# Router products turned over and spread on four column groups, the second routing stage rearranged between engines, two sets of FFN accumulators

## The chip, the core and the metric

The kernel runs on one core of a Trainium2 chip. Its time is the device time of one execution in microseconds (us), from several runs; a profile of one more execution gives a trace with the start and duration of every instruction. The engines are PE (TensorE, matrix products), DVE (VectorE), ACT (ScalarE), POOL (GpSimd) and SP (SyncE, which here only issues DMA transfers). PEld is PE's weight load.

## The reference

```python
x = L0_attn_x                                   # 8 x 1024 x 256
x = x + 0.5 * _L0_ffn_ref(_layernorm(x), router_w, w1, w2)
x = x + _L0_attn_ref(_layernorm(x), Wq, bq, Wk, bk, Wv, bv, Wp, bp)   # 16 heads of 16, rope, causal
x = x + 0.5 * _L0_ffn_ref(_layernorm(x), router_w, w1, w2)

def _L0_ffn_ref(x, router_w, w1, w2):           # 8192 tokens, 8 experts of capacity 1024
    logits = x_flat @ router_w
    expert_idx = argmax(softmax(logits)); gate = the probability of that expert
    pos = running count of tokens of the same expert; keep = pos < 1024
    expert_in[expert_idx, pos] += x_flat * keep
    hidden = gelu(expert_in @ w1[e]); expert_out = hidden @ w2[e]
    return expert_out[expert_idx, pos] * gate * keep
```

## The kernel before, in words

Five stages follow each other, each a block that all engines enter and leave together: first routing (`first_route_block`, names `r1_`), first FFN (`ffn_block`, `f1`), attention (`attention_block`, `at_`), second routing (`second_route_block`, `r2_`), second FFN (`f2`). Each engine runs its own program; semaphores order them. The trace writes `r_` and `f_` for either stage. A batch is 1024 tokens (8 tiles of 128); there are 8 batches, and a quarter q of a batch is two tiles.

**Routing.** For a batch b, DVE's `measure` takes mean and variance, POOL's `invert_std` finds 1/std by Newton steps, `normalize` writes `xn`, PE transposes it (`xt_ps`), ACT copies that to `xt`, and PE's `router(b, q)` multiplies: xt as the stationary operand, router_w (8 columns) moving, four fp32 products a quarter. DVE's `choose` picks the expert, PE's `count` makes running counts, DVE's `place_rows` computes the row number of each token and signals `rows_ready`, and POOL's `scatter(b)` sends the 8 tiles with an indirect DMA each to `expert_in`.

**Second routing** does the attention's output projection first. Attention leaves unnormalised outputs and their sums in DRAM (`o_rows`). At its start the sums of all batches are loaded (L588), inverted (L838) and stored (L593); then per batch SP's `load_o(b)` (L577) brings 1 MB of outputs to `o_in[b % 2]`, `load_inverses(b)` (L585) brings the inverses, each repeated over 16 rows, to the one buffer `o_inv`, POOL's `scale(b)` (L610) multiplies the two, ACT's `high` (L717) and DVE's `low` (L763) split the product into two fp32r parts for each half batch, PE's `project` (L655) multiplies, and DVE's `add` (L769) adds to x. `load_inverses(b)` waits for `scale(b - 1)`, `load_o(b)` for both `low` of batch b - 2. In the loop over b the work on batches b + 2 and b + 3 (add, low, scale) stands between the steps of routing for b and b - 1: POOL's order is `invert_std(b + 1)`, `scale(b + 3)`, `scatter(b - 1)`. DVE's `normalize` (L793) is there too.

**FFN.** 16 blocks of 512 rows, two an expert. In a block, for f in 0..7, PE runs `up(b, f)` (six products into `hid_ps`, L1084), ACT gelu and the high part, DVE the low part (L1037), and PE, two steps later, `down(b, f)` (twelve products into four accumulators `y_ps`, L1099). DVE's `combine(b)` (L1015) reads the accumulators after the block's last `down`; it stands in DVE's program after the low part f = 1 of the next block, and PE's first `down` of the next block waits for it:

```python
                pe.wait_ge(hid_lo_ready, FC * b + f + 1)
                if f == 0 and b >= 1:
                    pe.wait_ge(y_ready, b)
```

**Attention** runs 32 groups (four a batch), 12 steps t each, with PE, DVE (row maxima, L1525 and L1528) and ACT (exponentials) in a ring of three PSUM banks.

Of the kernel before, what the change touches and what calls it, by code (L numbers as in the profile page):

```python
# [14 lines left out]
F32 = mybir.dt.float32  # L15
# [13 lines left out]
E, CAP, F = 8, 1024, 1024  # L29
FC = F // P  # L30
# [165 lines left out]
def first_route_block(nc, sh, dr, w):  # L196
# [6 lines left out]
    with ExitStack() as ctx:  # L203
# [17 lines left out]
        xt = [sb(f"xt{k}", [P, TPQ, CC, P], F32) for k in range(2)]  # L221
# [14 lines left out]
        logit_ps = [ps(f"logit_ps{k}", [P, TPB, E]) for k in range(2)]  # L236
# [4 lines left out]
        x_loaded = [sem(f"x_loaded{b}") for b in range(B)]  # L241
# [8 lines left out]
        xt_used = sem("xt_used")  # L250
# [11 lines left out]
        def _(sp):  # L262
            def load_x(b):
                sp.dma_start(sh.x[:, TPB * b:TPB * (b + 1), 0:C],
                             dr["x"][b * S:(b + 1) * S, :].rearrange("(t p) c -> p t c", p=P)
                             ).then_inc(x_loaded[b], 16)
# [6 lines left out]
            sp.dma_start(sh.router[:], dr["router_w"].rearrange("(c p) e -> p c e", p=P)).then_inc(constants_loaded, 16)  # L273
# [44 lines left out]
        def _(pe):  # L318
            def router(b, q):
                n = QPB * b + q  # L320
                pe.wait_ge(xt_ready, n + 1)
                if q == 0 and b >= 2:
# [22 lines left out]
            for b in range(B):  # L345
                for q in range(QPB):
# [9 lines left out]
                    if q >= 1:  # L356
                        router(b, q - 1)
                    if q == 2 and b >= 1:
                        count(b - 1)
                router(b, QPB - 1)  # L360
# [3 lines left out]
        def _(act):  # L364
            def exponentials(b):
# [5 lines left out]
            for b in range(B):  # L371
                for q in range(QPB):
                    n = QPB * b + q
                    act.wait_ge(xt_ps_ready, n + 1)
                    if n >= 2:
                        act.wait_ge(xt_used, n - 1)
                    nc.scalar.copy(xt[q % 2][:], xt_ps[q % 2][:]).then_inc(xt_ready, 1)
                if b >= 1:
                    exponentials(b - 1)
            exponentials(B - 1)  # L380
# [3 lines left out]
        def _(dve):  # L384
# [15 lines left out]
            def measure(b):  # L400
                m, at = b // 2, per_pair * (b // 2) + 2 * (b % 2)
                dve.wait_ge(x_loaded[b], 16)
# [24 lines left out]
            def choose(b):  # L427

                k = b % 2
                dve.wait_ge(xt_used, QPB * (b + 1))  # L430
                link(v.tensor_reduce(best[:], logit_ps[k][:], AX.X, ALU.max))
                if b >= 2:
                    dve.wait_ge(exp_ready, b - 1)
                v.tensor_tensor(less[k][:], logit_ps[k][:], wide(best), ALU.subtract).then_inc(less_ready, 1)
# [53 lines left out]

def second_route_block(nc, sh, dr, w):
# [6 lines left out]
    with ExitStack() as ctx:  # L496
# [18 lines left out]
        half = [sb(f"half{k}", [P, TPB], F32) for k in range(2)]  # L515
        bits = sb("bits", [P, TPB], I32)
# [3 lines left out]
        sums = xn[:].rearrange("p a j c -> p (a j c)")  # L520
        assert TOK * H == P * 2 * TPQ * C
        xt = [sb(f"xt{k}", [P, TPQ, CC, P], F32) for k in range(2)]
        less = [sb(f"less{k}", [P, TPB, E], F32) for k in range(2)]
        work = [sb(f"work{k}", [P, TPB, E], F32) for k in range(2)]
        hot = sb("hot", [P, TPB, E], F32)
        onehot = [sb(f"onehot{k}", [P, TPB + 1, E], BF16) for k in range(2)]
        counts = sb("counts", [P, TPB, E], F32)
# [10 lines left out]
        logit_ps = [ps(f"logit_ps{k}", [P, TPB, E]) for k in range(2)]  # L538
# [22 lines left out]
        xt_used = sem("xt_used")  # L561
# [11 lines left out]
        def _(sp):  # L573
# [14 lines left out]
            sp.dma_start(sums, dr["o"].rearrange("(n v) t -> n v t", v=VW)[:, D, :]).then_inc(sums_loaded, 16)  # L588
            sp.dma_start(wp[:], dr["wp_t"].rearrange("(c p) o -> p c o", p=P)).then_inc(wp_loaded, 16)
            load_o(0)  # L590
            load_o(1)
            sp.wait_ge(sums_inverted, 1)
            sp.dma_start(dr["inv_sums"], sums).then_inc(sums_stored, 16)  # L593
            sp.wait_ge(sums_stored, 16)
# [1366 lines left out]
```

## Time and profile before

| | us |
|---|---|
| median of three runs (lowest to highest) | 2720.24 (2717.07 to 2720.41) |
| the profiled execution's own time | 2707.74 |
| its span, first to last instruction | 2706.0 |
| first routing | 0 to 145.9 |
| first FFN and attention | 145.9 to 2010.0 |
| second routing | 2012.2 to 2275.7 |
| second FFN | 2275.7 to 2706 |
| PE, DVE, ACT, POOL busy | 2227.9, 1699.0, 1218.6, 966.9 |

How to read it: a stage ends when its slowest engine does, so busy shares over the whole span say little; each stage has its own limit. Durations that this text uses come from the profiled execution.

### The profile page before, as it was taken

To read this page: it belongs to the slowest core of one execution; us is meant where nothing else is said; L and a number is where in the kernel's file an instruction comes from. 1 tells how busy PE (TensorE), PEld (TensorE's weight loads), DVE (VectorE), ACT (ScalarE), POOL (GpSimd) and SP (SyncE) were. 2 spreads that over 40 slices of the span, in tenths; PEclk is the share of its full clock that TensorE was granted. 3 is DMA by queue.
4 is the path that set the end of the run, shared out by engine and by line. 5 is a ranking of instruction groups with operands and counts; after the bars stand their busy time and mean duration, and the time that the engine had idled before them with its cause. 6 is when DMAs were issued, how large, how long until landed. Compare 5 with 4: busy or idle time off the path is not lost. (4 is left out here: it accounts for less than half of the span.)

```text
span 2706.0 us, 43185 instructions
## 1 busy us (share of the span) xinstructions
PE 2227.9 (82%) x14740; PEld 1451.9 (54%) x14740; DVE 1699.0 (63%) x5181; ACT 1218.6 (45%) x2442; POOL 966.9 (36%) x1344
## 2 busy tenths in 40 slices
PE   6659999935699999999999999999962664899997
PEld 6658888834334444444444444443322664788886
DVE  7435555433477877877878878877733663555552
ACT  1224444411056665665666665666750212344443
POOL 3723434326423333333333333330002564333442
PEclk9999999965589999999999999999986775999999
DMA  9552223021524434435344344344315424323220
GB/s 341 187 197 96 88 71 104 29 73 58 132 64 110 117 84 111 112 86 130 87 110 114 86 97 111 80 105 99 80 60 124 144 69 165 126 71 100 77 71 22
DMA packets 185131, 283.21 MB, mean 105 GB/s; under 512 B 14392, under 2 KB 147704, under 8 KB 176720
## 3 DMA queue, kind: packets, MB, share of 16 engines
q1 hardware_dynamic: 170576, 247.08, 34.0%
q0 software_dynamic: 14336, 33.38, 3.5%
q8 instruction: 117, 1.92, 0.3%
q14 instruction: 102, 0.84, 0.1%
HBM read 153.99 MB, written 126.88 MB: 104 GB/s over the span
## 5 line engine op out<-in xcount | busy, mean ns | idle before, releaser
L1646 ACT ACTIVATE at_probs<-at_score_ps 128x512 f32<-128x512 f32 (+3 forms) x1536 | 692.9, 497 | 451.6 <-PE at_score_ps L1763 312.6
L1525 DVE CUSTOM_DVE_ANT_0 at_junk<-at_max_ps,at_causal 128x128 f32<-128x128 f32 (+3 forms) x1024 | 485.5, 484 | 128.2 <-PE at_max_ps L1749 126.2
L1749 PE MATMUL at_max_ps<-at_k,at_q 96*128 96x512 bf16 (+3 forms) x1536 | 494.1, 341 | 43.1 <-DVE at_peak L1525 30.7
L1760 PE MATMUL at_score_ps<-at_q,at_k 99*128 99x512 bf16 (+3 forms) x1536 | 499.3, 332 | 10.7 <-DMA at_v<-v_rows 4.4
L1528 DVE TENSOR_REDUCE at_peak<-at_max_ps 128x1 f32<-128x512 f32 x512 | 352.4, 688 | 118.2 <-PE at_max_ps L1749 114.9
L1037 DVE TENSOR_TENSOR f_hid_lo<-f_hid,f_hid_hi 128x512 fp32r<-128x512 f32 x256 | 177.5, 693 | 322.8 <-ACT f_hid_hi L1061 322.2
L1749 PEld LDWEIGHTS at_max_ps<-at_k,at_q 96*128 96x128 bf16 x1536 | 144.6, 98 | 398.0 <-DVE at_peak L1525 192.0
L1058 ACT ACTIVATE f_hid<-f_hid_ps 128x512 f32<-128x512 f32 x256 | 153.3, 599 | 413.7 <-PE f_hid_ps L1084 413.5
L1773 PE MATMUL at_o_ps<-at_probs,at_v 128*32 128x512 f32 (+3 forms) x3072 | 337.8, 512 | 1.2 <-ACT at_probs L1646 0.7
L1099 PE MATMUL f_y_ps<-f_w_hi,f_hid_hi 128*128 128x256 f32 x1024 | 292.7, 286 | 47.4 <-DVE f_xe L1015 28.9
L1099 PE MATMUL f_y_ps<-f_w_hi,f_hid_lo 128*128 128x256 f32 x1024 | 291.4, 285 | 0.0
L1099 PE MATMUL f_y_ps<-f_w_lo,f_hid_hi 128*128 128x256 f32 x1024 | 290.2, 283 | 0.0
L960 POOL TENSOR_SCALAR f_xn<-f_xe 128x256 f32<-128x256 f32 x120 | 164.3, 1376 | 217.3 <-PE f_xt_ps L1072 168.0
L1099 PEld LDWEIGHTS f_y_ps<-f_w_hi,f_hid_hi 128*128 128x128 f32 x1024 | 194.2, 190 | 70.4 <-issue 41.2
L1368 POOL TENSOR_TENSOR at_by_cos<-at_qk,at_cos 128x512 f32<-128x512 f32 x64 | 70.4, 1100 | 437.0 <-DVE at_qk L1484 437.0
L1763 PE MATMUL at_score_ps<-at_hide_bf,ident_bf 128*128 128x128 bf16 x1024 | 226.1, 223 | 0.0
L1760 PEld LDWEIGHTS at_score_ps<-at_q,at_k 99*128 99x128 bf16 x1536 | 150.9, 99 | 126.0 <-ACT at_probs L1646 73.7
L1099 PEld LDWEIGHTS f_y_ps<-f_w_lo,f_hid_hi 128*128 128x128 f32 x1024 | 194.1, 190 | 9.0
L1099 PEld LDWEIGHTS f_y_ps<-f_w_hi,f_hid_lo 128*128 128x128 f32 x1024 | 194.0, 189 | 0.0
L1084 PE MATMUL f_hid_ps<-f_xt_hi,f_w_hi 128*128 128x512 f32 x512 | 168.3, 410 | 2.8 <-DVE f_xt_lo L1006 2.8
L1061 ACT CAST f_hid_hi<-f_hid 128x512 fp32r<-128x512 f32 x256 | 158.8, 620 | 8.2
L1084 PE MATMUL f_hid_ps<-f_xt_lo,f_w_hi 128*128 128x512 f32 x512 | 162.4, 398 | 0.0
(175 smaller groups left out, 3631.0 us busy)
## 6 DMA issues: line engine op xcount, KB each, us to landing
f_w_raw<-in_w SPq DMA_DIRECT2D x32, 1024.0 KB, 7.6
qk<-at_parts SPq DMA_DIRECT2D x32, 768.0 KB, 4.2
expert_in<-r_zeros SPq DMA_DIRECT2D x16, 1040.0 KB, 11.3
f_xe<-expert_in SPq DMA_DIRECT2D x32, 520.0 KB, 7.3
v_rows<-at_v_outs SPq DMA_DIRECT2D x32, 512.0 KB, 6.2
at_v<-v_rows SPq DMA_DIRECT2D x32, 512.0 KB, 10.4
o_rows<-at_o_out SPq DMA_DIRECT2D x64, 256.0 KB, 2.0
at_q<-qk SPq DMA_DIRECT2D x32, 384.0 KB, 7.6
```

The source lines that it names most:

```text
L960: last = nc.gpsimd.tensor_scalar(xn[:, t, :], x[:, t, 0:C], x[:, t, MEAN:MEAN + 1], x[:, t, RSTD:RSTD + 1], ALU.subtract, ALU.mult)
L1037: v.tensor_tensor(hid_lo[f % NHID][:], hid[f % NHID][:], hid_hi[f % NHID][:].bitcast(F32), ALU.subtract).then_inc(hid_lo_ready, 1)
L1061: nc.scalar.copy(hid_hi[f % NHID][:], hid[f % NHID][:]).then_inc(hid_hi_ready, 1)
L1084: last = nc.tensor.matmul(hid_ps[f % 2][:], w[ws][:, cc, f * P:(f + 1) * P], x[b % 2][:, cc, :], start=(i == 0), stop=(i == 3 * CC - 1))
L1099: last = nc.tensor.matmul(y_ps[t][:], a[m][:, rows], w[ws][:, f, :], start=(f == 0 and i == 0), stop=(f == FC - 1 and i == 2))
L1525: v.tensor_tensor_reduce(junk[bank(k, r)][:, 0:w], src, causal[:, HALF - w:HALF], 1.0, LEAST, ALU.add, ALU.max, out).then_inc(max_used, 1)
L1528: v.tensor_reduce(out, src, AX.X, ALU.max).then_inc(max_used, 1)
L1646: a.activation(probs[t % 2][:, h, c0:c0 + w], score_ps[(GH * t + h) % BANKS][:, 0:w], ACT.Exp, scale=float(SCALE)).then_inc(exp_done, 1)
L1749: te.matmul(max_ps[bank(u, r)][:, 0:w], q[u][0:ROWS, h, i * P:(i + 1) * P], kk[u][0:ROWS, h, k0:k0 + w], start=True, stop=True).then_inc(m ...
L1760: last = te.matmul(out[:, 0:w], kk[u][:, h, j * P:(j + 1) * P], q[u][:, h, hf * HALF + c0:hf * HALF + c0 + w], start=True, stop=not diagonal)
L1763: last = te.matmul(out[:, 0:P], sh.ident_bf[:], hide_bf[:], start=False, stop=True)
L1773: last = te.matmul(o_ps[h * VW:(h + 1) * VW, c0:c0 + w], vv[u][:, j, h, :], probs[t % 2][:, h, c0:c0 + w], start=(t == FIRST_STEP[hf]), st ...
```

## The change

In both routings the product is turned over: router_w, padded to 32 columns (`EW`), is the stationary operand, xt moves (256 columns a quarter), and the four quarters of a batch use four column groups of PE (`tile_position`), writing 32 partitions each of `turned_ps`. ACT copies it (`turn`), and two PE transposes bring the logits back. `xt` holds a whole batch. In the second routing `scale` moves from POOL to DVE, `normalize` from DVE to ACT (as x * rstd + shift, with `shift` computed on POOL), and the sums of batches 0 to 6 are inverted during attention. The FFN has two sets of accumulators.

```diff
@@ both routings, PE
-            def router(b, q):
...
-                for j in range(TPQ):
-                    for cc in range(CC):
-                        last = nc.tensor.matmul(logit_ps[b % 2][:, TPQ * q + j, :], xt[q % 2][:, j, cc, :],
-                                                sh.router[:, cc, :], start=(cc == 0), stop=(cc == CC - 1))
-                last.then_inc(xt_used, 1)
+            def router(b):
+                pe.wait_ge(xt_ready, QPB * (b + 1))
+                if b >= 1:
+                    pe.wait_ge(turned_ready, b)
+                for cc in range(CC):
+                    for q in range(QPB):
+                        last = nc.tensor.matmul(turned_ps[q * EW:(q + 1) * EW], router_w[:, cc, :],
+                                                xt[:, q, :, cc, :], start=(cc == 0), stop=(cc == CC - 1),
+                                                tile_position=(0, q * EW))
+                last.then_inc(turned_ps_ready, 1)
+
+            def logits(b):
+                pe.wait_ge(turned_ready, b + 1)
...
+                for j in range(TPQ):
+                    last = nc.tensor.transpose(logit_ps[b % 2][:, j].rearrange("p q e -> p (q e)"),
+                                               turned[:, j], sh.ident[:])
@@ second_route_block, SP
-            sp.dma_start(dr["inv_sums"], sums).then_inc(sums_stored, 16)
-            sp.wait_ge(sums_stored, 16)
-            load_inverses(0)
-            load_inverses(1)
+            sp.dma_start(inverses_of(dr, B - 1), sums[:]).then_inc(sums_stored, 16)
             for b in range(2, B):
                 sp.wait_ge(y_lo_ready, 2 * (b - 1))
                 load_o(b)
+                if b == B - 1:
+                    sp.wait_ge(sums_stored, 16)
                 load_inverses(b)
@@ second_route_block, POOL
-            def scale(b):
...
+                nc.gpsimd.tensor_tensor(shift[k][:], less_mean[k][:], rstd[k][:].bitcast(F32), ALU.mult)
@@ second_route_block, ACT
+            def normalize(n):
...
+                for a in range(TPQ):
+                    j = TPQ * q + a
+                    last = nc.scalar.activation(xn[:, q % 2, a, :], tile_of(sh.x, TPB * b + j), ACT.Identity,
+                                                bias=shift[k][:, j:j + 1], scale=rstd[k][:, j:j + 1].bitcast(F32))
@@ second_route_block, DVE
+            def scale(b):
+                k = b % 2
+                dve.wait_ge(o_loaded[k], 16 * CC * (b // 2 + 1))
+                dve.wait_ge(inv_loaded, 16 * CC * (b + 1))
+                v.tensor_tensor(o_in[k][:], o_in[k][:], o_inv[:], ALU.mult).then_inc(y_scaled, 1)
@@ ffn_block
-        y_ps = [ps(f"y_ps{k}", [P, C]) for k in range(TPK)]
+        y_ps = [[ps(f"y_ps{k}_{a}", [P, 2, C]) for a in range(TPK // 2)] for k in range(2)]
...
-                if f == 0 and b >= 1:
-                    pe.wait_ge(y_ready, b)
+                if f == 0 and b >= 2:
+                    pe.wait_ge(y_ready, b - 1)
@@ attention_block, SP and DVE
+                done = g // NG - 1
+                if done >= 0 and g % NG == 1:
+                    for half in range(2):
+                        sp.wait_ge(o_stored[half], 16 * NG * (done + 1))
+                    sp.wait_ge(sums_stored, 16 * done)
+                    sp.dma_start(sums[:], sums_of(dr, done)).then_inc(sums_loaded, 16)
+                if done >= 0 and g % NG == 3:
+                    sp.wait_ge(sums_inverted, done + 1)
+                    sp.dma_start(inverses_of(dr, done), sums[:]).then_inc(sums_stored, 16)
...
+                    if t == 8 and g >= NG and g % NG == 2:
+                        dve.wait_ge(sums_loaded, 16 * (g // NG))
+                        v.reciprocal(sums[:], sums[:]).then_inc(sums_inverted, 1)
```

SP's queue at the start of the second routing, before (all sums are inverted, stored and read back before the first inverses can be loaded):

```order
L588 DMA r_xn<-o_rows 128x1024
L589 DMA r_wp<-in_wp_t 128x2x256
L577 DMA r_o_in<-o_rows 128x1x1024 x4
L593 DMA inv_sums<-r_xn 128x1024 [waits r2_sums_inverted]
L585 DMA r_o_inv<-inv_sums 128x1x1024 [waits r2_sums_stored]
L585 DMA r_o_inv<-inv_sums 128x1x1024
```

The same place after the change:

```order
L624 DMA r_o_in<-o_rows 128x1x1024 x2
L632 DMA r_o_inv<-inv_sums 128x1x1024 x2
L637 DMA r_wp<-in_wp_t 128x2x256
L638 DMA r_router_w<-in_router_w 128x2x32
L639 DMA r_sums<-o_rows 128x1x128
L624 DMA r_o_in<-o_rows 128x1x1024 x2
L632 DMA r_o_inv<-inv_sums 128x1x1024 [waits r2_y_scaled]
```

The outputs and inverses of batch 0 are now the first four transfers, with no wait ahead of them.

DVE in the loop of the second routing, before, from the end of one batch's statistics (`r_rstd`) on; `r_xn` is `normalize`, `r_best` begins `choose`:

```order
L128 TENSOR_SCALAR r_rstd<-r_bits 128x8 [waits r2_step]
L783 COPY x_sb<-r_moments 128x8
L793 TENSOR_SCALAR r_xn<-x_sb,r_moments,r_rstd 128x256 [waits r2_xt_ps_ready,r2_rstd_ready]
L793 TENSOR_SCALAR r_xn<-x_sb,r_moments,r_rstd 128x256
L793 TENSOR_SCALAR r_xn<-x_sb,r_moments,r_rstd 128x256 [waits r2_xt_ps_ready]
L793 TENSOR_SCALAR r_xn<-x_sb,r_moments,r_rstd 128x256
L801 TENSOR_REDUCE r_best<-r_logit_ps 128x8 [waits r2_xt_used]
L804 TENSOR_TENSOR r_less<-r_logit_ps,r_best 128x64 [waits r2_link_step]
```

The same place after the change:

```order
L129 TENSOR_SCALAR r_rstd<-r_bits 128x8 [waits r2_step]
L866 COPY x_sb<-r_moments 128x8
L841 TENSOR_TENSOR r_o_in<-r_o_in,r_o_inv 128x2048 [waits r2_inv_loaded,r2_o_loaded1]
L873 TENSOR_REDUCE r_best<-r_logit_ps 128x8 [waits r2_logits_ready]
L876 TENSOR_TENSOR r_less<-r_logit_ps,r_best 128x64 [waits r2_link_step]
```

The eight `normalize` instructions of a batch are gone from DVE, and one product of 2048 columns, which waits for two transfers, stands ahead of `choose`.

## Rows read from the trace of the kernel before

**Rows 1.** What PE's products into y_ps waited for, both FFNs (us, times)

```profile
  DVE f_xe L1015: 28.9, 30
```

**Rows 2.** Timeline, second FFN: start us, us, engine, line, operation, [idle before]

```profile
2396.25 0.63 PE L1084 MATMUL f_hid_ps<-f_xt_hi,f_w_hi 128*128 128x512 f32 x2
...
2399.08 0.63 PE L1084 MATMUL f_hid_ps<-f_xt_hi,f_w_hi 128*128 128x512 f32 x2
...
2399.81 1.65 DVE L1015 SCALAR_TENSOR_TENSOR f_xe<-f_y_ps,f_xe 128x256 f32<-128x256 f32 x4
...
2401.61 0.36 PE L1099 MATMUL f_y_ps<-f_w_hi,f_hid_hi 128*128 128x256 f32 x1 [0.97 <-DVE f_xe L1015]
...
2401.96 0.69 DVE L1037 TENSOR_TENSOR f_hid_lo<-f_hid,f_hid_hi 128x512 fp32r<-128x512 f32 x1 [0.50 <-ACT f_hid_hi L1061]
...
2403.11 0.62 PE L1084 MATMUL f_hid_ps<-f_xt_hi,f_w_hi 128*128 128x512 f32 x2
...
2407.75 0.28 PE L1099 MATMUL f_y_ps<-f_w_hi,f_hid_hi 128*128 128x256 f32 x1
```

**Rows 3.** Timeline of POOL, second routing: scale, scatter and invert_std

```profile
2044.52 4.49 POOL L610 TENSOR_TENSOR r_o_in<-r_o_in,r_o_inv 128x2048 f32<-128x2048 f32 x1 [57.94 <-DMA r_o_inv<-inv_sums]
...
2060.21 4.50 POOL L610 TENSOR_TENSOR r_o_in<-r_o_in,r_o_inv 128x2048 f32<-128x2048 f32 x1 [11.20 <-DMA r_o_inv<-inv_sums]
...
2191.47 4.56 POOL L610 TENSOR_TENSOR r_o_in<-r_o_in,r_o_inv 128x2048 f32<-128x2048 f32 x1
2201.20 1.08 POOL L623 DMA_INDIRECT expert_in<-x_sb,scatter_row  x1 [5.16 <-DVE scatter_row L832]
...
2211.26 0.24 POOL L137 TENSOR_TENSOR r_tmp<-r_rstd 128x8 f32<-128x8 f32 x1
...
2215.21 0.20 POOL L616 COPY x_sb<-r_rstd 128x8 f32<-128x8 f32 x1
...
2250.87 2.87 POOL L623 DMA_INDIRECT expert_in<-x_sb,scatter_row  x1 [0.30 <-DVE scatter_row L832]
2254.04 1.90 POOL L623 DMA_INDIRECT expert_in<-x_sb,scatter_row  x1 [0.30 <-issue]
...
2267.72 0.97 POOL L623 DMA_INDIRECT expert_in<-x_sb,scatter_row  x1 [0.30 <-issue]
```

**Rows 4.** Stretches of second routing: busy by engine, clock, DMA share, GB/s

```profile
2052.00:2060.00 8.00, 6.95 (x48) 6.74 (x46) 1.85 (x3) 0.00 (x0) 0.00 (x0) 0.82 0.52 124
...
2106.00:2108.00 2.00, 0.99 (x9) 0.78 (x7) 0.35 (x1) 1.43 (x3) 0.54 (x1) 1.00 0.14 16
...
2149.00:2166.00 17.00, 7.61 (x45) 7.51 (x46) 13.87 (x51) 3.09 (x6) 9.64 (x16) 0.60 0.59 181
```

**Rows 5.** Timeline of DVE around the second routing

```profile
2015.94 6.55 DVE L838 RECIPROCAL r_xn<-r_xn 128x1024 f32<-128x1024 f32 x1 [3.49 <-DMA r_xn<-o_rows]
...
2120.28 4.42 DVE L793 TENSOR_SCALAR r_xn<-x_sb,r_moments,r_rstd 128x256 f32<-128x256 f32 x2
...
2197.15 1.23 DVE L763 TENSOR_TENSOR r_y_lo<-r_o_in,r_y_hi 128x1024 fp32r<-128x1024 f32 x1 [5.93 <-ACT r_y_hi L717]
...
2200.32 1.28 DVE L769 TENSOR_TENSOR x_sb<-x_sb,r_y_ps 128x512 f32<-128x512 f32 x2
...
2202.65 2.70 DVE L775 BATCH_NORM_STATS2 r_stats<-x_sb 128x6 f32<-128x256 f32 x8
...
2250.61 2.28 DVE L191 TENSOR_TENSOR f_w_lo<-f_w_raw,f_w_hi 128x2048 fp32r<-128x2048 f32 x1
```

**Rows 6.** Timeline of POOL, first routing

```profile
49.95 1.19 POOL L302 DMA_INDIRECT expert_in<-x_sb,scatter_row  x1 [5.50 <-DMA expert_in<-r_zeros]
...
137.87 0.98 POOL L302 DMA_INDIRECT expert_in<-x_sb,scatter_row  x1 [0.30 <-issue]
```

**Rows 7.** A stretch of attention, columns as in rows 4

```profile
1300.00:1400.00 100.00, 92.07 (x653) 41.80 (x651) 79.34 (x257) 58.58 (x129) 36.05 (x68) 0.97 0.47 109
```

**Rows 8.** Costliest groups of the page: busy, mean ns | idle before, releaser

```profile
L1749 PE MATMUL at_max_ps<-at_k,at_q 96*128 96x512 bf16 (+3 forms) x1536 | 494.1, 341 | 43.1 <-DVE at_peak L1525 30.7
```

More of the change, by code:

```diff
@@ L235, in first_route_block @@
         xt_ps = [ps(f"xt_ps{k}", [P, TPQ, CC, P]) for k in range(2)]
[L236 removed]
+        turned_ps = ps("turned_ps", [QPB * EW, TPQ, P])
+        logit_ps = [ps(f"logit_ps{k}", [P, TPQ, QPB, EW]) for k in range(2)]
         count_ps = ps("count_ps", [P, TPB + 1, E])
@@ L364, in _, with turn @@
         def _(act):
+            def turn(b):
+                act.wait_ge(turned_ps_ready, b + 1)
+                if b >= 2:
+                    act.wait_ge(logits_ready, b - 1)
+                nc.scalar.copy(turned[b % 2][:], turned_ps[:]).then_inc(turned_ready, 1)
             def exponentials(b):
@@ L515, in second_route_block @@
         half = [sb(f"half{k}", [P, TPB], F32) for k in range(2)]
+        less_mean = [sb(f"less_mean{k}", [P, TPB], F32) for k in range(2)]
+        shift = [sb(f"shift{k}", [P, TPB], F32) for k in range(2)]
         bits = sb("bits", [P, TPB], I32)
@@ L729, in _ @@
                     high(b, h)
+            normalize(0)
+            normalize(1)
             for b in range(B):
@@ L836, in _ @@
                 v.memset(onehot[k][:], 0.0)
-            dve.wait_ge(sums_loaded, 16)
-            v.reciprocal(sums, sums).then_inc(sums_inverted, 1)
+            scale(0)
             dve.wait_ge(wp_hi_ready, 1)
@@ L845, in _ @@
                     add(b, q)
+                    if b == 1 and q == 0:
+                        scale(2)
                     if q % 2:
@@ L849, in _ @@
             for b in range(B):
-                ahead = b + 2 < B
-                normalize(b, 0)
-                normalize(b, 1)
+                if b + 3 < B:
+                    scale(b + 3)
                 if b >= 1:
                     choose(b - 1)
-                for q in range(2):
-                    normalize(b, 2 + q)
-                    if ahead:
-                        add(b + 2, q)
+                if b + 2 < B:
+                    add(b + 2, 0)
+                    add(b + 2, 1)
                 if b + 3 < B:
@@ L862, in _ @@
                     place_rows(b - 1)
-                if ahead:
-                    for q in range(2, QPB):
-                        add(b + 2, q)
-                    if b + 3 < B:
-                        low(b + 3, 1)
+                if b + 2 < B:
+                    add(b + 2, 2)
+                    add(b + 2, 3)
+                if b + 3 < B:
+                    low(b + 3, 1)
+                if b + 2 < B:
                     measure(b + 2)
@@ L1098, in down @@
                     for i, (a, w) in enumerate(((hid_hi, w2_hi), (hid_hi, w2_lo), (hid_lo, w2_hi))):
-                        last = nc.tensor.matmul(y_ps[t][:], a[m][:, rows], w[ws][:, f, :],
-                                                start=(f == 0 and i == 0), stop=(f == FC - 1 and i == 2))
+                        last = nc.tensor.matmul(y_ps[b % 2][t // 2][:, t % 2, :], a[m][:, rows], w[ws][:, f, :],
+                                                start=(f == 0 and i == 0 and t % 2 == 0),
+                                                stop=(f == FC - 1 and i == 2), skip_group_check=True)
                 last.then_inc(hid_free, 1)
```

207 lines of the change are left out of this document (125 added, 82 removed).

## The prediction

> **What bounds the kernel now.** I read the stages apart, first the timeline, then waits and stretches.
>
> *FFNs.* The waits of the products into y_ps put 28.9 us on DVE's `combine`, 30 times: once a block but the first, in both FFNs [rows 1]. The timeline shows one [rows 2]: `combine` (four reads, 1.65 us) begins when the last `down` of the old block is through, and PE, which has nothing else in its program, starts the next `down` only at 2401.61. From one `up` to the next PE takes 2399.08 - 2396.25 = 2.83 us in a plain step and 2403.11 - 2399.08 = 4.03 us in this one, 1.20 us more. Otherwise PE runs without gaps here, so PE is the bound and this wait is on its path.
>
> *First routing.* POOL's first scatter starts at 49.95, released by the transfer that clears `expert_in`; the 64th starts at 137.87 [rows 6]. Between them POOL issues one every 1.28 us and does one `invert_std`; its gaps before them are 0.3 us. So POOL and the clearing are the bound, not PE.
>
> *Second routing.* `scale(0)` cannot start before 2044.52, since the inverses come by way of DRAM; `scale(1)` starts at 2060.21, after another wait for inverses, `scale(7)` at 2191.47, done at 2196.0 [rows 3]. In the middle POOL goes round: `scale` 4.56, a wait of 5.16 for `place_rows` (which stands behind the low part made from that same product), eight scatters in 2211.26 - 2201.20 = 10.1, `invert_std` in 2215.41 - 2211.26 = 4.15 us: 24 us a batch. After `scale(7)` come five batches' scatters; the stage's last instruction on POOL ends at 2268.7, 72.6 us after `scale(7)`.
>
> *The transfers of this stage.* While outputs or inverses are on their way, with hardly another transfer, the DMA share is 0.52 at 124 GB/s [rows 4]: half of the 16 engines. That stays 0.52 when loads of both kinds are in flight, so they use the same half. One load is 1.05 MB: 1.05 / 0.124 = 8.5 us. In the 17 us of 2149 to 2166 one of each kind went by together with a batch's scatters (181 GB/s, share 0.59), so two loads take 17.3 us and the scatters add nothing. I take 8.65 us a load, 17.3 us a batch: below the 24 us of now, and next in line.
>
> *Attention.* PE 92% busy, DVE 79%, clock 0.97 [rows 7].
>
> **The change, part by part.**
>
> *Accumulators.* PE waits for `combine` of two blocks before, long done. 30 x 1.20 = -36 us. What is late next? PE reaches the third `down` of the block at 2407.75 - 1.20 = 2406.55, and its low part begins at 2401.96 and takes 0.69 [rows 2], 3.9 us of slack. Bounds: -29 (the 0.97 us that the trace calls idle, 30 times) and -36. I take -36, from start to start.
>
> *First routing.* Fewer PE records (8 turned products and 2 transposes instead of 32 products a batch), an ACT copy more. PE, ACT and DVE all work ahead of POOL, whose own list is unchanged: 0, bounds -1 to +1.
>
> *Start of the second routing.* Inverses of batch 0 lie in DRAM already. Loads o0 and i0 (outputs, inverses) are the first in the queue at 2012.2; about 2 us until data move, 17.3 us, so `scale(0)` starts near 2032 instead of 2044.5.
>
> *`scale` on DVE.* Not shown there; nearest is DVE's difference of 128x2048 fp32 from SBUF, 2.28 us [rows 5]; bounds 2.28 and the 4.56 of POOL. I take 2.3, the same shape and kind.
>
> *`normalize` on ACT* of 128x256: not shown; by the stretch 2149 to 2166 ACT is busy 3.09 of 17 us [rows 4], and eight more of at most the 0.6 us of a 128x512 copy are 5. Hidden by ACT's idle time; uncovered it would cost 5 us a batch.
>
> *DVE's load a batch.* Adds 4 x 0.64, low parts 2 x 1.22, statistics 2.70 and some 1.8 of small ones, `choose` 1.3, `place_rows` 2.3, all by [rows 5] and the instructions between them, and `scale` 2.3: 15.4 us, under 17.3.
>
> *POOL's load a batch.* 10.1 + 4.15 + 0.3 (`shift`) = 14.6. POOL and DVE disturb each other: under POOL's `scale` two `normalize` instructions took 4.42 us together [rows 5], and under DVE's 2.28 us differences two scatters took 2.87 and 1.90 instead of 0.97 [rows 3]. So a DVE product with both inputs in SBUF costs POOL about 1 us; `scale` and two low parts, 3 us: 17.6 us, level with the transfers.
> The Trainium skill ("SBUF — State Buffer", Who interferes with whom) says that the port pair shared by these two is locked and the loser is blocked entirely. By that rule POOL would lose the whole 4.7 us of the three and go at 19.3 us a batch, six us later at the end. The trace, with about 1 us lost of 2.28, speaks for less.
>
> *So the stage goes at the pace of its transfers.* Sixteen loads, 16 x 8.65 = 138.4; small ones 1; the weights of expert 0, which use these engines too: between `scale(1)` at 2060.2 (its inverses landed) and the first gap of DMA near 2107 [rows 3, 4] five loads went by, 47 - 43.3 = 4. From 2012.2: + 2 + 138.4 + 1 + 4 = 2157.6, + 0.3 + 2.3 gives the end of `scale(7)` at 2160.3, where it was 2196.0: -35.7. The tail: `place_rows(3)` about 8.2 us after `scale(7)` (choose, two adds, high and low, the count behind a projection at low clock), then five batches of scatters 5 x 10.2, two `invert_std` with shift 8.9, 2.8 lost to the weights' differences, 1 to a low part: 72 us, as now 72.6. I take -35 for the stage. Bounds: nothing lost at all to DVE, -40; DVE or POOL setting a pace of 21 us, -15 (four batches 3.7 us slower, and 5 in the tail).
>
> *Attention.* Seven reciprocals of 128x128, an eighth of the 6.55 us one [rows 5]: 0.82 us each, 5.7 in all; 14 small transfers, under a share of 0.47 [rows 7]. SP issues each load more than a group ahead of DVE's need. DVE has a fifth of its time free, but PE waited 30.7 us in all for DVE's maxima [rows 8], so some of it shows. Bounds 0 and +6; I take +3.
>
> **Sum:** -36 + 0 - 35 + 3 = -68 on a span of 2706.0: 2638. The profiled execution took 2707.7, 12.5 under the median of the runs, 2720.2; I give the time against the median: 2652.
>
> **Rivals.**
> A (0.56): as above, 2652, own range 2640 to 2664.
> B (0.28): the second routing goes at 20 to 22 us a batch, because DVE's `scale` at the head of its loop waits for transfers and all its 13 us of work then waits for PE at the low clock, or because of the shared port. For it: the 15.4 us of DVE hold no waits, and the sums of DVE and POOL lie within 2 us of 17.3. Against it: in 2149 to 2166 DVE was busy 13.87 of 17. -36 - 15 + 3: 2672.
> C (0.08): the reciprocals hide and nothing is lost on the port: -36 - 40 + 0: 2644.
> D (0.05): the FFN's wait only moves (to the next low part behind `combine`, or to gelu): 0 to -10 of the -36. 2683. Against it stand the 3.9 us of slack.
> E (0.03): slower than before. One mechanism: DVE stands in attention at the wait for the sums, whose load SP issues behind a wait of its own; all row maxima, and with them PE, stand too. It decides from 68 / 7 = 10 us an event on; at 12 us the time is 2733. Against it: the load is asked for in the middle of one group and needed late in the next, some 40 us later, and SP's other stores land in 2 us.
>
> **How the numbers follow.** The predicted time is A's. A, B and C cover 2640 to 2680; with the bounds of the FFN (-29) and of the stage I give 2637 to 2680. A measurement of this kernel tells 0.2% (5 us) from no change; all but E lie well beyond: faster 0.96, same 0.01, slower 0.03.
>
> **What would show each step right or wrong.** Products into y_ps wait for nothing at a block's start, and blocks come every 23.5 us instead of 24.7. `scale(0)` on DVE near 2017, which is 2032 less the 18 us saved in the first FFN and with attention's 3; seven `scale` steps about 18 us apart, each ended by a wait for inverses, DMA share 0.5 and more throughout (A); scales not waiting for DMA and 20 us or more apart (B). First scatter of the first routing still at 50 us. Attention longer by 0 to 6 us. The prediction is wrong if the loads do not keep 124 GB/s when issued back to back, or if the low clock on PE stretches DVE's loop past 17.3 us.

## The result, and the profile after

| | before | after |
|---|---|---|
| median of the runs beside each other (lowest to highest) | 2719.99 (2717.07 to 2720.41) | 2648.66 (2646.14 to 2651.83) |
| the profiled execution's own time, its span | 2707.74, 2706.0 | 2647.95, 2646.2 |

The ratio is 0.9741 (95% interval 0.9724 to 0.9757). The forecast was 2652 in a range of 2637 to 2680.

Each stage begins with its first transfer in SP's queue. Timeline of SP, kernel after (start us, us, queue, line, transfer):

```profile
160.19 0.92 SPq L1014 DMA_DIRECT2D f_xe<-expert_in  x2
573.64 0.36 SPq L1383 DMA_DIRECT2D x_sb<-x  x1
2004.99 1.36 SPq L624 DMA_DIRECT2D r_o_in<-o_rows  x2
2234.10 0.93 SPq L1014 DMA_DIRECT2D f_xe<-expert_in  x2
```

Before, the same transfers started at 145.94, 576.74, 2012.20 and 2275.66. So by stage:

| us | first routing | first FFN | attention | second routing | second FFN | span |
|---|---|---|---|---|---|---|
| before, profiled execution | 145.9 | 430.8 | 1435.5 | 263.5 | 430.3 | 2706.0 |
| after, profiled execution | 160.2 | 413.4 | 1431.4 | 229.1 | 412.1 | 2646.2 |
| difference | +14.3 | -17.4 | -4.1 | -34.4 | -18.2 | -59.8 |

The spans differ by 59.8 us, the medians by 71.3. Two kernels below that contain the first routing of before (E1 and E2) say where the rest lies: it took 160.4 and 160.6 us there, in executions whose time matches their medians. The profiled execution of before, 12 us below its median, was fortunate in that stage, so the +14.3 is no cost of the change.

**FFN.** Timeline of the kernel after, second FFN, the place of [rows 2]:

```profile
2353.68 0.63 PE L1161 MATMUL f_hid_ps<-f_xt_hi,f_w_hi 128*128 128x512 f32 x2
...
2354.40 1.65 DVE L1092 SCALAR_TENSOR_TENSOR f_xe<-f_y_ps,f_xe 128x256 f32<-128x256 f32 x4
...
2356.50 0.62 PE L1161 MATMUL f_hid_ps<-f_xt_hi,f_w_hi 128*128 128x512 f32 x2
2356.55 0.69 DVE L1114 TENSOR_TENSOR f_hid_lo<-f_hid,f_hid_hi 128x512 fp32r<-128x512 f32 x1 [0.50 <-ACT f_hid_hi L1138]
```

The step with `combine` in it takes 2356.50 - 2353.68 = 2.82 us, as long as a plain one ([rows 2]: 2.83). Who waited for `combine`, all 128 instructions of it (us, times):

```profile
  POOL x L1047: 154.3, 16
  POOL out L1047: 153.9, 16
  DVE f_xe L1092: 4.5, 2
```

PE is no longer among them ([rows 1] had 28.9 us, 30 times).

**Second routing.** `scale`, timeline of DVE after:

```profile
2019.87 2.29 DVE L841 TENSOR_TENSOR r_o_in<-r_o_in,r_o_inv 128x2048 f32<-128x2048 f32 x1 [14.64 <-DMA r_o_inv<-inv_sums]
...
2031.61 2.29 DVE L841 TENSOR_TENSOR r_o_in<-r_o_in,r_o_inv 128x2048 f32<-128x2048 f32 x1 [5.11 <-DMA r_o_inv<-inv_sums]
...
2047.15 2.29 DVE L841 TENSOR_TENSOR r_o_in<-r_o_in,r_o_inv 128x2048 f32<-128x2048 f32 x1
...
2060.87 2.29 DVE L841 TENSOR_TENSOR r_o_in<-r_o_in,r_o_inv 128x2048 f32<-128x2048 f32 x1 [2.44 <-DMA r_o_inv<-inv_sums]
...
2074.41 2.29 DVE L841 TENSOR_TENSOR r_o_in<-r_o_in,r_o_inv 128x2048 f32<-128x2048 f32 x1
...
2092.57 2.28 DVE L841 TENSOR_TENSOR r_o_in<-r_o_in,r_o_inv 128x2048 f32<-128x2048 f32 x1
...
2114.38 2.29 DVE L841 TENSOR_TENSOR r_o_in<-r_o_in,r_o_inv 128x2048 f32<-128x2048 f32 x1
...
2136.17 2.28 DVE L841 TENSOR_TENSOR r_o_in<-r_o_in,r_o_inv 128x2048 f32<-128x2048 f32 x1
```

The forecast had 17.3 us from each to the next, with a wait for inverses each time. Measured: 11.7, 15.5, 13.7 and 13.5, then 18.2, 21.8 and 21.8, the last four without such a wait. So transfers do not set the later pace. One period of 21.8 us, from the first scatter of a batch to that of the next, is closed by these rows. POOL, after:

```profile
2108.75 1.08 POOL L667 DMA_INDIRECT expert_in<-x_sb,scatter_row  x1 [6.30 <-DVE scatter_row L906]
...
2115.27 2.24 POOL L667 DMA_INDIRECT expert_in<-x_sb,scatter_row  x1 [0.31 <-issue]
...
2120.08 0.22 POOL L138 TENSOR_TENSOR r_tmp<-r_rstd 128x8 f32<-128x8 f32 x1
...
2124.05 0.20 POOL L660 COPY x_sb<-r_rstd 128x8 f32<-128x8 f32 x1
2130.54 1.07 POOL L667 DMA_INDIRECT expert_in<-x_sb,scatter_row  x1 [6.29 <-DVE scatter_row L906]
```

ACT, after:

```profile
2124.28 1.09 ACT L791 ACTIVATE r_xn<-x_sb,r_shift,r_rstd 128x256 f32<-128x256 f32 x2 [5.98 <-POOL x_sb L660]
2125.28 0.24 ACT L778 ACTIVATE r_wp<-r_less 128x64 f32<-128x64 f32 x1
2125.42 1.03 ACT L766 CAST r_y_hi<-r_o_in 128x1024 fp32r<-128x1024 f32 x1
```

DVE, after:

```profile
2126.48 1.23 DVE L845 TENSOR_TENSOR r_y_lo<-r_o_in,r_y_hi 128x1024 fp32r<-128x1024 f32 x1 [7.46 <-ACT r_y_hi L766]
...
2129.58 0.17 DVE L906 CAST scatter_row<-r_row 128x8 int32<-128x8 f32 x1
```

Eight scatters, 11.3 us; `invert_std(b + 1)`, 4.2; ACT's first `normalize`, then `exponentials(b - 1)` and `high`, which stand behind it in ACT's program, 2.2; `low` and `place_rows(b - 1)`, 3.1; 1.0 until the next scatter: 21.8. POOL waits 6.3, ACT 6.0 and DVE 7.5 us in the same period. Each waits for the others in turn, and no single one is the bound.

The tail, from the end of `scale(7)` at 2138.45 to POOL's last scatter, took 88.7 us. First scatters of batches 3, 4 and 7, POOL:

```profile
2152.34 1.07 POOL L667 DMA_INDIRECT expert_in<-x_sb,scatter_row  x1 [6.30 <-DVE scatter_row L906]
...
2170.79 1.07 POOL L667 DMA_INDIRECT expert_in<-x_sb,scatter_row  x1 [4.22 <-DVE scatter_row L906]
...
2215.01 2.26 POOL L667 DMA_INDIRECT expert_in<-x_sb,scatter_row  x1 [5.55 <-DVE scatter_row L906]
```

The same chain goes on there: batch 3 starts 13.9 us after `scale(7)` (8.2 were forecast), and POOL waits 4.2 us before each of the next two batches and 5.6 us before the last. The forecast had no such waits.

### The profile page after: what moved, and what is told of

Same layout as the page of the kernel before. It is cut to its first block and busy times, and to the rows that moved or that the text cites. A ratio compares the mean times of both kernels' runs of the same rounds, so it can differ in the third digit from the quotient of the medians.

```text
span 2646.2 us, 42777 instructions
## 1 busy us (share of the span) xinstructions
PE 2167.2 (82%) x14516; PEld 1376.1 (52%) x14516; DVE 1692.4 (64%) x5140; ACT 1254.5 (47%) x2522; POOL 942.7 (36%) x1344
## 5 line engine op out<-in xcount | busy, mean ns | idle before, releaser
L1843 PE MATMUL at_max_ps<-at_k,at_q 96*128 96x512 bf16 (+3 forms) x1536 | 493.2, 340 | 42.9 <-DVE at_peak L1616 31.3
L1037 POOL TENSOR_SCALAR f_xn<-f_xe 128x256 f32<-128x256 f32 x120 | 164.0, 1374 | 183.7 <-PE f_xt_ps L1149 133.5
```

The costliest lines, as they stand in the source:

```text
L1037: last = nc.gpsimd.tensor_scalar(xn[:, t, :], x[:, t, 0:C], x[:, t, MEAN:MEAN + 1], x[:, t, RSTD:RSTD + 1], ALU.subtract, ALU.mult)
L1843: te.matmul(max_ps[bank(u, r)][:, 0:w], q[u][0:ROWS, h, i * P:(i + 1) * P], kk[u][0:ROWS, h, k0:k0 + w], start=True, stop=True).then_inc(m ...
```

## The experiments

Times are medians. Since the medians of before differ from one group of runs to the next (2713.4 to 2720.0), kernels are compared by their ratio to the runs of before beside them; 0.001 is 2.7 us. The changed kernel has 0.9741.

| | median | ratio (interval) | stage touched, us |
|---|---|---|---|
| E1 before + pairs | 2678.57 | 0.9856 (0.9831 to 0.9881) | FFNs 413.1 and 412.3 |
| E2 first routing undone | 2649.18 | 0.9748 (0.9726 to 0.9770) | first routing 160.6 |
| E3 normalize ahead there | 2652.22 | 0.9761 (0.9738 to 0.9783) | first routing 158.3 |
| E4 one column group there | 2664.91 | 0.9799 (0.9774 to 0.9824) | first routing 174.8 |
| E5 exponentials first | 2631.08 | 0.9688 (0.9672 to 0.9705) | second routing 212.2 |
| E6 old router, second | 2655.44 | 0.9761 (0.9740 to 0.9782) | second routing 236.7 |
| E7 scale on POOL | 2666.27 | 0.9810 (0.9794 to 0.9826) | second routing 247.7 |
| E8 sums late | 2679.49 | 0.9863 (0.9847 to 0.9880) | second routing 255.3 |
| E9 inversions five times | 2679.58 | 0.9883 (0.9866 to 0.9900) | attention 1468.8 |
| E10 measure first as well | 2627.01 | 0.9679 (0.9665 to 0.9693) | second routing 224.3 |
| E11 loads apart | 2671.30 | 0.9850 (0.9836 to 0.9864) | second routing 254.9 |
| E12 normalize on DVE | 2634.61 | 0.9719 (0.9705 to 0.9733) | second routing 221.7 |

In kernels that leave it untouched the second routing takes 229.1 to 233.7 us (the kernel after and E2 to E4) and 239.1 in E9, whose profiled execution was its slowest; this is the noise to hold against.

**E1.** The part of the diff with `y_ps` and `y_ready`, applied to the kernel before.

> The kernel before with only the two pairs of accumulators. The theory of the prediction: each of the 30 waits of 1.20 us goes and nothing else moves, so 36 us less than before, about 2684 us (ratio 0.987), and the stretch of each FFN 18 us shorter; the first routing stays at 146 us. Rival: part of the 36 us belongs to other changes, and this kernel gains less than 30. It also gives a second trace of the first routing, the attention and the second routing as they were before.

The ratio takes 39 us off (32 to 46), the FFN stretches lose 17.7 and 18.0. The term holds and nothing else belongs to it. What is new is the first routing, unchanged from before, at 160.4 us where 146 was expected. POOL in it, kernel E1:

```profile
49.85 1.19 POOL L302 DMA_INDIRECT expert_in<-x_sb,scatter_row  x1 [6.03 <-DMA expert_in<-r_zeros]
...
77.05 1.13 POOL L302 DMA_INDIRECT expert_in<-x_sb,scatter_row  x1 [2.56 <-DVE scatter_row L462]
...
103.80 1.04 POOL L302 DMA_INDIRECT expert_in<-x_sb,scatter_row  x1 [3.70 <-DVE scatter_row L462]
...
152.40 0.97 POOL L302 DMA_INDIRECT expert_in<-x_sb,scatter_row  x1 [0.30 <-issue]
```

Five batches wait 2.6 to 3.8 us for `place_rows`; the last scatter starts at 152.40, where [rows 6] had 137.87. The code is the same, and so is the granted clock (1.00 in both). What differs is a wait of ACT for PE's transposes. Waits between 40 and 150 us, E1 (us in all, times, longest):

```profile
ACT r_xt L377 <- remote: 34.3, 6, 8.8
...
POOL expert_in L302 <- DVE scatter_row L462: 16.8, 5, 3.8
```

The profile writes "remote" where it finds no record that ended near the signal; the signal here is PE's, and it came long after the end of PE's record. The profiled execution of before has no such wait, and 0.6 us, twice, in the second row. So the execution that was 14.5 us faster in this stage is the one in which PE's results were never late; the last section comes back to this.

**E2.** The first routing of before in the changed kernel.

> The changed kernel with the first routing as it was before (router products not turned over there). In the trace after the change this stage is 14.25 us longer (160.2 instead of 145.9), with waits of about 4 us on POOL before each batch's scatters. Theory R (the turned-over product makes a ring normalize, transposes, router, turn, logits, choose, count, place_rows, normalize that is longer than POOL's work): the stage returns to 146 us and the kernel is 14 us faster than the changed one, about 2635 us. Rival N (the 14 us are chance of one execution): no change, 2649 us.

Rival N: 0.9748 against 0.9741, 160.6 against 160.2 us. Turning the products over neither costs nor gains there. It does take work and clock from PE. The stretch from 40 to 140 us, columns as in [rows 4], kernel after, then E2:

```profile
40.00:140.00 100.00, 39.64 (x285) 26.27 (x285) 49.41 (x214) 21.33 (x40) 60.92 (x78) 0.60 0.55 208
```

```profile
40.00:140.00 100.00, 70.81 (x383) 67.46 (x383) 50.06 (x219) 19.49 (x35) 60.50 (x80) 1.00 0.55 207
```

PE is busy 39.6 us instead of 70.8, and its granted clock is 0.60 on average instead of 1.00.

**E3.**

```diff
@@ first_route_block, DVE
+            normalize(0)
             for b in range(B):
-                normalize(b)
+                if b + 1 < B:
+                    normalize(b + 1)
                 if b >= 1:
                     choose(b - 1)
```

> The changed kernel, but in the first routing DVE does normalize of batch b + 1 before choose and place_rows of batch b - 1. Theory R (a ring through DVE's order): the ring opens, POOL sets the pace again (10.2 us a batch), the stage takes about 146 us, and the kernel is 14 us faster than the changed one, about 2635 us. Rival L (PE itself falls behind after the turned-over products: semaphores of its transposes and counts come 2 to 11 us later than its records): the stage stays above 155 us, and less than 5 us is gained.

158.3 us and 0.9761: theory R falls, DVE's order is not what makes POOL wait. Rival L's number holds; why PE's results come late is the subject of the last section.

**E4.**

```diff
@@ first_route_block, PE
-                for cc in range(CC):
-                    for q in range(QPB):
-                        last = nc.tensor.matmul(turned_ps[q * EW:(q + 1) * EW], router_w[:, cc, :],
-                                                xt[b % 2][:, q, :, cc, :], start=(cc == 0), stop=(cc == CC - 1),
-                                                tile_position=(0, q * EW))
+                for q in range(QPB):
+                    for cc in range(CC):
+                        last = nc.tensor.matmul(turned_ps[:, q], router_w[:, cc, :],
+                                                xt[b % 2][:, q, :, cc, :], start=(cc == 0), stop=(cc == CC - 1),
+                                                skip_group_check=True)
...
```

> The changed kernel, but in the first routing the turned-over products all use the first column group (32 partitions, eight products of one batch one after the other, eight transposes of 32 rows back instead of two of 128). Rival L (the delays of 2 to 11 us after PE's records come from the column groups): they vanish from the trace, and the stage is 5 to 14 us shorter although the products themselves take 1 to 3 us longer a batch. Theory R (ring and low clock, column groups innocent): the ring grows by 1 to 3 us a batch, the stage takes 167 to 180 us, and the kernel is 7 to 20 us slower than the changed one.

The stage is 14.6 us longer, as theory R had it, and rival L falls: between 40 and 150 us ACT still waits for late results of PE five times, 13.4 us in all (four times, 11.4 us in the kernel after). Timeline of PE, E4, one batch's router products:

```profile
114.39 5.24 PE L330 MATMUL r_turned_ps<-r_xt,r_router_w 128*32 128x256 f32 x16
```

The same sixteen records take 1.94 us on four groups (104.05 in the kernel after), at a granted clock of 0.50 where E4's row has 0.69. So column groups make the products 2.7 times as fast by these rows; no two rows at one clock were compared. The longer way through PE, and through ACT's copy of the result (1.00 us instead of 0.37), shows in the first routing: between 40 and 150 us POOL waits 24.7 us for `place_rows` instead of 17.0. The Trainium skill ("TensorE: Matmul & The Clock Gate", Part 3: Packing small matmuls) says that small products in different column groups run concurrently, with 2.38 times for three; by the rows above, the trace agrees.

**E5.**

```diff
@@ second_route_block, ACT
+                    if q == 2:
+                        if b >= 1:
+                            exponentials(b - 1)
+                        if b + 3 < B:
+                            high(b + 3, 0)
                     normalize(n + 2)
-                    if q == 2 and b >= 1:
-                        exponentials(b - 1)
-                    if q >= 2 and b + 3 < B:
-                        high(b + 3, q - 2)
+                    if q == 3 and b + 3 < B:
+                        high(b + 3, 1)
```

> The changed kernel, but in the second routing ACT does exponentials(b - 1) and the first high of batch b + 3 ahead of normalize for batch b + 1, instead of behind it. Theory C (a closed chain sets 21.8 us a batch: POOL's eight scatters, invert_std, ACT's first normalize, exponentials and high behind it, DVE's low and place_rows, the next scatters): the chain opens, POOL alone sets the pace with 15.5 to 17 us a batch, and four or five periods at 21.8 us become shorter by 5 us: 20 to 25 us less, about 2626 us. Rival T (transfers or DVE set the pace): less than 5 us gained, 2645 us.

14 us faster than the changed kernel by the ratios (5 to 23 by the ends of both intervals), the stage 17 us shorter; the 20 to 25 us expected were too much. Timeline of ACT, E5:

```profile
2096.04 0.26 ACT L778 ACTIVATE r_wp<-r_less 128x64 f32<-128x64 f32 x1
2096.19 1.03 ACT L766 CAST r_y_hi<-r_o_in 128x1024 fp32r<-128x1024 f32 x1
...
2104.09 1.09 ACT L791 ACTIVATE r_xn<-x_sb,r_shift,r_rstd 128x256 f32<-128x256 f32 x2 [6.86 <-POOL x_sb L660]
```

`exponentials` run 8 us ahead of the `normalize` they stood behind, and POOL's next scatter starts at 2104.49, after a wait of 0.44 us. In every second batch up to `scale(7)` POOL still waits 3.0 to 3.6 us for `place_rows`, which the expectation left out. Theory C holds in kind, and rival T (less than 5 us) falls. This kernel is faster than the kernels before and after.

**E6.** The router products and `choose` of before in the second routing; `scale`, `normalize` and the sums stay changed.

> The changed kernel with the router product of the second routing as it was before (not turned over, 32 small products a batch, count at q = 2); scale and normalize stay where the change put them. Theory C: the products are no link of the chain; PE is busier and its clock higher; within 6 us of the changed kernel. Rival G (the wait of ACT for the last turned product, 13.4 us in the changed kernel's trace, comes from the column groups): this wait goes and the last scatters come 5 to 6 us earlier, 2643 us.

5 us slower by the ratios with intervals that overlap, and 236.7 us for the stage is inside the 229.1 to 239.1 of the same code: no difference that can be told. Rival G falls: DVE's wait for the last logits is as long without column groups. Timeline of PE and DVE, E6:

```profile
2207.21 1.88 PE L712 MATMUL r_logit_ps<-r_router_w,r_xt 128*128 128x8 f32 x8 [1.08 <-issue]
2220.71 0.23 DVE L848 TENSOR_REDUCE r_best<-r_logit_ps 128x8 f32<-128x64 f32 x1 [13.86 <-remote]
```

**E7.** `scale` on POOL, between `invert_std(b + 1)` and `scatter(b - 1)`.

> The changed kernel with scale on POOL again (4.5 us instead of 2.3), between invert_std(b + 1) and scatter(b - 1) as before. Theory C: POOL is a link of the chain, and each of five or six batches takes 4.5 us more minus the 1.3 us that DVE's low no longer costs POOL: 15 to 25 us slower than the changed kernel, 2664 to 2674 us. Rival T (transfers set the pace): 0 to 5 us slower.

19 us slower by the ratios. Its last steps, timeline of POOL:

```profile
2137.86 4.51 POOL L676 TENSOR_TENSOR r_o_in<-r_o_in,r_o_inv 128x2048 f32<-128x2048 f32 x1
...
2161.72 4.50 POOL L676 TENSOR_TENSOR r_o_in<-r_o_in,r_o_inv 128x2048 f32<-128x2048 f32 x1
```

23.9 us apart, where the changed kernel has 21.8 (25.0 was expected): theory C, and rival T falls. 23.9 is also the late pace of the kernel before.

**E8.** No inversions in attention; all sums loaded, inverted and stored at the start of the second routing.

> The changed kernel without the inversions during attention: all sums are loaded, inverted and stored at the start of the second routing, as before. Before the change scale(0) began 32.3 us after the stage's first transfer was issued, after it 14.9 us. Theory: everything behind scale(0) is later by 17 us, attention gets back at most 4 us, so 13 to 17 us slower than the changed kernel, 2662 to 2666 us. Rival H (the start is hidden behind the chain on POOL, ACT and DVE): less than 5 us slower. Rival A (the seven inversions cost attention 6 us or more): under 10 us slower, with attention shorter by 6.

Twice what was expected: 33 us by the ratios, 26 by the stage. `scale(0)` started 31.3 us after the stage's first transfer (14.9 in the changed kernel), and the next steps were 13.6 and 20.0 us apart instead of 11.7 and 15.5, since loads behind the sums are late too. The expectation of 13 to 17 us missed that second part, and rivals H and A both fall. Attention took 1432.7 us without the inversions, no less than with them.

**E9.**

```diff
@@ attention_block, DVE
+                        for i in range(4):
+                            if g >= 2 * NG or i:
+                                dve.wait_ge(again, 4 * (g // NG - 1) + i)
+                            v.reciprocal(sums_again[:], sums[:]).then_inc(again, 1)
+                        dve.wait_ge(again, 4 * (g // NG))
                         v.reciprocal(sums[:], sums[:]).then_inc(sums_inverted, 1)
```

> The changed kernel with each of attention's seven reciprocals of 128x128 done five times (four go to a buffer that nobody reads): 28 more of 0.8 to 0.95 us, 23 to 27 us more work on DVE in attention. If DVE's free time there hides such work (the seven cost nothing that is seen): 0 to 6 us slower than the changed kernel. If most of it shows: 15 to 25 us slower, and the seven cost 4 to 6 us in the change.

39 us slower by the ratios (30 to 48) for 28 x 0.95 = 27 us of work: more than the whole of it shows, beyond either expectation. The profiled execution was this kernel's slowest (2693.43), so its 1468.8 us for attention say too much. One tile's instructions, E9 (ns minimum, median, maximum; first and last start):

```profile
L1686 DVE RECIPROCAL at_sums_again<-at_sums x28: 945/953/954, 1022.9 to 1999.2; 128x128 f32<-128x128 f32 x28
```

Yet the seven single ones do not show: attention took 1428.1 to 1435.4 us in ten traces with them (E9 apart), and 1426.9, 1432.7 and 1435.5 in the three without. Five in a row, 4.8 us, are not a fair measure of one of 0.95; that one hides in PE's and ACT's queues is an argument, not shown.

**E10.** E5, and besides `high(b + 3, 1)` ahead of `normalize` on ACT and `measure(b + 2)` ahead of `low(b + 3, 1)` on DVE.

> The kernel with exponentials and high ahead of normalize (212 us for the second routing, 229 in the changed one), and besides on ACT the second high of batch b + 3 ahead of normalize too, on DVE measure(b + 2) ahead of the second low of batch b + 3. POOL still waited there 3 to 4 us in every second batch, once for place_rows and once behind the statistics. If that wait is what is left of the chain: 8 to 14 us less than the kernel with exponentials first (2631), 2620 us. If the later low makes PE and the adds late instead: within 4 us of 2631, or slower.

0.9679 against E5's 0.9688, 2 us: no difference that can be told, and the 8 to 14 us of the first expectation are not there. Its profiled execution was its slowest (2639.14), so what it waited for is left open.

**E11.**

```diff
@@ second_route_block, SP
                 sp.wait_ge(y_lo_ready, 2 * (b - 1))
+                sp.wait_ge(inv_loaded, 16 * CC * b)
                 load_o(b)
+                sp.wait_ge(o_loaded[b % 2], 16 * CC * (b // 2 + 1))
```

> The changed kernel, but in the second routing SP issues the outputs of batch b (from 2 on) only when the inverses before them have landed, and the inverses only when those outputs have: never two kinds in flight together. The prediction took 8.65 us a load whether alone or together, and so 17.3 us a batch; in that case this edit costs only the latencies, and scale steps come every 20 us or more in either kernel. Theory O (two loads in flight together move 200 GB/s where one alone moves 124): scale(3) and scale(4) come 4 to 8 us later each than in the changed kernel, where they came 13.7 and 13.5 us after the one before; the chain behind them hides a part, so 5 to 20 us slower in all, 2654 to 2669 us.

30 us slower by the ratios, above theory O's range. `scale(2)` and `scale(3)` came 24.3 and 24.7 us after the step before. That it pays to have loads in flight together is shown, and the 20 us or more that the prediction's price gave "in either kernel" is not what the changed kernel did (13.7 and 13.5). Stretches, columns as in [rows 4]: two of E11 in which only outputs were in flight, then the kernel after with both kinds:

```profile
2058.00:2064.00 6.00, 3.82 (x24) 3.52 (x22) 4.83 (x15) 4.49 (x8) 0.00 (x0) 0.78 0.52 124
...
2100.00:2104.00 4.00, 1.72 (x8) 1.75 (x9) 3.86 (x10) 1.19 (x2) 0.00 (x0) 0.50 0.48 180
```

```profile
2052.00:2060.00 8.00, 4.05 (x19) 4.05 (x20) 6.19 (x25) 4.69 (x8) 3.31 (x13) 0.61 0.51 208
```

SP's issues that belong to the second of these, E11:

```profile
2098.05 1.20 SPq L624 DMA_DIRECT2D r_o_in<-o_rows  x2
2106.59 1.20 SPq L632 DMA_DIRECT2D r_o_inv<-inv_sums  x2
```

About the same DMA share carried 124, 180 and 208 GB/s. But theory O's reason, that one load alone moves 124 and two together 200, does not hold: 180 is a stretch with one kind alone, and the 124 of [rows 4], 2052 to 2060, is one with both. There the inverses had been issued at 2049.03 and landed just before 2060.21, and SP's next issue in the kernel before was

```profile
2052.51 1.20 SPq L577 DMA_DIRECT2D r_o_in<-o_rows  x2
```

What sets the bytes within a share stays open, and so does how E11's 30 us divide between that and the time from an issue to the first data, which E11 pays for each load by itself.

**E12.** `normalize` back on DVE, in the places of before, with `scale` between its second and third quarter.

> The changed kernel with normalize of the second routing on DVE again (eight instructions of 0.33 us at least a batch, in the places of before), scale on DVE too. Theory C: ACT no longer waits for 1/std ahead of exponentials and high, so the chain of 21.8 us opens; DVE has 15.4 + 2.7 to 4.4 = 18 to 20 us a batch and sets the pace: 5 to 15 us less than the changed kernel, 2634 to 2644 us. Rival D (taking normalize off DVE was needed: DVE is the bound and its waits add up): slower than the changed kernel by 5 us or more.

6 us faster than the changed kernel by the ratios (the intervals overlap, 0.9724 to 0.9733), the stage 7.4 us shorter. Theory C's direction holds, at the low end, and rival D falls: `scale` steps are 18.2 to 19.4 us apart late in the loop, where DVE's own work was put at 18 to 20.

## Why the prediction came out right, and where it was wrong

The time, 2649 for 2652, is right. The mechanism is right for the accumulators, the largest term. For the second routing it is not, and that its sum came out is luck.

- **Accumulators, -36.** Right: -17.4 and -18.2 in the traces, and alone by E1. The slack behind it was there: PE's waits on `down` for low parts are 37.7 us before and 40.2 after, four times in both.
- **First routing, 0.** Right in size (E2), not in reason. "PE, ACT and DVE all work ahead of POOL" described one fortunate execution. In others POOL waits for `place_rows` (E1), and E4 shows that PE's latency counts. The 12.5 us between the profiled execution and the median, which I carried over as an offset, lie in this stage, by E1 and E2: as far as these two tell, a stage of about 160 us stands in both medians, so the offset was fair, though I didn't know why.
- **`scale` on DVE, 2.3.** Right, 2.29.
- **Start of the stage.** Put at 19.8 us after its first transfer, was 14.9; E8 undoes it and loses 26 us of stage.
- **"So the stage goes at the pace of its transfers", 8.65 us a load.** This step failed. It read the DMA share of [rows 4] as a capacity: 0.52 with one kind in flight, 0.52 with two, "so they use the same half". The kernel after moved 208 GB/s at a share of 0.51, and E11 between 124 and 180 with one kind alone. The term was mis-sized: with both kinds in flight, `scale` came every 13.7 and 13.5 us, under 7 us a load.
- **`normalize` on ACT, "hidden by ACT's idle time".** This step failed too, and it is the one that costs. Its work, four pairs of 1.09 us, is within the 5 us estimated. But the first waits for POOL's 1/std, and `exponentials` and `high` are queued behind it, which `place_rows` and so POOL wait for. I named no one queued behind that new wait. E5 takes it away and wins 14 us; E12, which takes it away too but loads DVE, wins 6.
- **The two errors offset each other.** `scale(7)` was done at 2138.5, 133.5 us after the stage's start (148.1 forecast), and the tail was 88.7 us (72 forecast), by the chain's waits. Sum: -34.4 in this pair of traces; by the others of the same code 232.5 to 239.1 us against 263, -24 to -31, for -35.
- **POOL and DVE on the port.** Put at 3 us a batch. The scatter at 2115.27, issued under `scale`, took 2.24 instead of 0.97: 1.3 us a batch. Of the two low parts one ran while POOL waited, the other beside scatters of 1.07 and 1.00. The scatter began 0.89 us into `scale`, and its 1.27 us more are nearly the 1.40 us that `scale` then still took. My rows said the same, and I misread them: the scatter at 2250.87 [rows 3] lost 1.90 us, where the difference under it [rows 5] still took 2.02. The Trainium skill ("SBUF — State Buffer", Who interferes with whom) calls the shared port pair an exclusive lock. In these rows the trace agrees with it, and not with the lesser loss that I argued for. The same section of the Trainium skill says that its probe saw no `tensor_tensor` stall a DMA; here `scale`, which is one, held up an indirect DMA.
- **Attention, +3.** Not seen, 0 within about 4 us.
- **Rivals.** B's pace of 20 to 22 us did appear, in three of the seven periods from scatters to scatters (two of the seven steps of `scale`), and by another chain than DVE's queue behind `scale`. D and E have nothing for them: no new wait on `down` and no stand in attention.

## What to carry to other kernels

When an instruction moves to an idle engine, list what it waits for and what stands behind it in that program: idle time hides work, not a wait. A DMA busy share is not a capacity: here one of about a half went with 124 to 208 GB/s, so it doesn't say that transfers are the bound. Ask instead who waited for a transfer. And compare the profiled execution with the median before trusting that a stage has slack: here one stage took 145.9 us in one execution and 160.4 in another, with the same code.

## What the runs showed of the hardware

In every trace but one, PE's results reached the other engines late at times while POOL issued scatters, in both routings and with the old products as well as the turned-over ones. The one is the profiled execution of before, where it happened in neither routing though POOL issued the same 128 scatters: so scatters beside them are not enough for it. In the first routing E1, the same code, had it six times on ACT, and took 14.5 us longer. Timeline of PE and ACT in E2's first routing, four transposes and the copy of their result:

```profile
110.10 1.09 PE L354 MATMUL r_xt_ps<-ident,r_xn 128*128 128x128 f32 x4
...
113.92 0.59 ACT L378 COPY r_xt<-r_xt_ps 128x512 f32<-128x512 f32 x1 [4.90 <-remote]
```

The copy could have started at 111.2: in the profiled execution of before such a copy started 1.1 us after its transposes did. At the end of the second routing it is longest. PE and ACT, kernel after:

```profile
2194.48 1.94 PE L716 MATMUL r_turned_ps<-r_xt,r_router_w 128*32 128x256 f32 x16 [0.41 <-issue]
...
2207.83 0.37 ACT L772 COPY r_wp<-r_turned_ps 128x256 f32<-128x256 f32 x1 [13.40 <-remote]
```

From the end of the records to their reader are 11.4 us here, and 11.6 in E6, with sixteen scatters in a row on POOL beside them. The longest such wait in the stage's last 70 us was 3.7 us in E5, 2.8 in E10, 7.1 in E12, 6.8 in E1, 8.5 in E11, 9.4 in E9, and 10.7 to 13.9 in the others (E2 to E4, E6 to E8). The edits of E5 and E12 were not made for it, and what part of their gain is due to it is not told apart. It isn't the column groups alone (E2 and E6 have it without them), nor DVE's order (E3), nor a low clock of PE, which was granted in full in E2's first routing. Its cause stays open.
